# One quad of edges in four loaded from GpSimd's queue instead of SP's, in a graph layer on one core

## The chip, the core and the metric

The kernel runs on one core of a Trainium2 chip. Its time is the device time of one execution, in microseconds (us), taken as the median of several runs. Profiles come from one further execution, recorded by the hardware profiler.

## What is computed

The layer updates 12,500 nodes of 128 features. 200,000 edges of 128 features each are summed into the node that the edge points to (`dst`, sorted ascending), and a three-layer perceptron with a closing LayerNorm runs on every node:

```
agg = segment_sum(edge_attr, dst, num_segments=12500)      # 200000 x 128 -> 12500 x 128
h   = relu(layernorm(x))
h   = concat([h, agg]); h = relu(h @ W1 + b1); h = relu(h @ W2 + b2); h = h @ W3 + b3
out = x + layernorm(h) * ln_w + ln_b
```

All of it is fp32. The edges are 102.4 MB of the 116.5 MB that move.

## The kernel before

**Quads.** The edges are read once, in order, in 130 quads (`QUADS`) of 1,536 edges. A quad is 786,432 bytes and is loaded by two transfers of 384.0 KB (`load_quad`, line 344), each in rows of 1,536 bytes, into one of eight slots of `ring` (`RING = 8`). Quad q lies in slot q modulo 8. Each slot has its own semaphore, `edges_loaded[slot]`, which rises by 32 for a whole quad.

**What is done with a quad.** TensorE multiplies its rows with a one-hot matrix of VectorE (`seg`, line 497, 24 matmuls), which sums the edges of each node inside windows of 32. ScalarE copies the sums (`copy_part`). GpSimd makes a placement matrix (`placement`, line 899) that says at which rows the windows lie, TensorE applies it (`put`, line 508), and VectorE adds the result to `agg` (`add`, line 1065). `place` has two buffers, so the placement of quad q waits until the put of quad q-2 is done (`pool.wait_ge(placed, q - 1)`).

**Steps.** The nodes are worked on in groups of 384. The main loop has 31 steps (`STEPS`). Step i takes four quads, 4i+6 to 4i+9 (`AHEAD = 6`), and layers 1 to 3 of node group i between them: TensorE runs layer 1 on the sums, then seg and put of one quad, layer 2, seg and put, layer 3, seg and put, the x part of the next layer 1, seg and put, and the transposes of the group two ahead. The put that follows seg of quad q is that of quad q-1. The loop of each engine is written out by hand in that order, and the engines meet by semaphores alone.

**The queues.** SP issues every load of edges and of x and nearly all stores, in program order on one queue. In a step it issues the x rows of group i+4 (192.0 KB, line 339), then four quads, 4i+14 to 4i+17, each as `reload`: a wait until the quad that held the slot has gone through seg (`seg_done >= q - 7`), then the two transfers. From step i = 3 on it adds after each quad a store of 24.0 KB (`store_part`, line 379, 13 groups in eighths); the other groups are stored at the end, two at a time (line 384). ScalarE issues only the weights at the start and the last small pieces of the output.

**GpSimd.** It has issued no transfer so far. In a step it copies the window bases of four quads (`rows_of`, line 890), makes four placements, and adds a bias to x of group i+2 (`bias_x`, line 907). At the start it zeroes `agg` (line 884). Its step reads:

```
rows_of(4 * i + AHEAD, 4, True)
for k in range(4):
    placement(4 * i + AHEAD + k, k, k, i + 2)
if more_x:
    bias_x(i + 2)
```

Of the kernel before, what the change touches and what calls it, by code (L numbers as in the profile page):

```python
# [38 lines left out]
HALF = QC // 2  # L39
# [23 lines left out]
RING = 8  # L63
HALF_RING = RING // 2
# [14 lines left out]
AHEAD = 6  # L79
# [3 lines left out]
STEPS = GROUPS - 1  # L83
ROUNDS = (STEPS - 3) // 2
STORED_EARLY = 13
WTS = 6 * 16


def gnn_kernel(nc, x, dst, edges, w1, b1, w2, b2, w3, b3, lnw, lnb, out):
    assert CHUNKS * NODES_PER_CHUNK - SLACK >= TAIL_BASE and GROUPS == 32 and QUADS == 4 * STEPS + AHEAD and LAST_P * LAST_PER == LAST_N and LAST_P <= P and TOP_QUADS * QC == (ROWT - 1) * P and 0 < FIRST_OF_LAST <= LROW and RC * RP == REST  # L90
    with ExitStack() as ctx:
# [3 lines left out]
        def sem(name):  # L95
            return ctx.enter_context(nc.semaphore(name))
# [111 lines left out]
        edges_loaded = [sem(f"edges_loaded{k}") for k in range(RING)]  # L208
        onehot_ready = sem("onehot_ready")
        seg_done = sem("seg_done")  # L210
# [8 lines left out]
        pool_went_on = sem("pool_went_on")  # L219
# [40 lines left out]
        def half_of_edges(q, k):  # L260

            return edges[bass.ds(q * QUAD + k * (QUAD // 2), QUAD // 2), :].rearrange("(s p j) f -> p s (j f)", p=P, j=PER)

        def ring_slot(k):
            return ring[:, k, :].rearrange("p (s e) -> p s e", s=QC)
# [53 lines left out]
        with nc.Block() as block:  # L319
# [3 lines left out]
            def _(sp):  # L323
# [11 lines left out]
                def load_x(g, par, before):  # L335

                    if not (isinstance(before, int) and before == 0):
                        sp.wait_ge(x_loaded[par], 16 * before)
                    sp.dma_start(xg(g), group_rows(x, g)).then_inc(x_loaded[par], 16)  # L339

                def load_quad(q, slot):

                    for k in range(2):
                        sp.dma_start(ring_slot(slot)[:, k * HALF:(k + 1) * HALF, :], half_of_edges(q, k)).then_inc(edges_loaded[slot], 16)  # L344
# [4 lines left out]
                load_x(0, 0, 0)  # L349
                load_x(1, 1, 0)  # L350
                sp.dma_start(tail_e[:, :, :], edges[TAIL0:EDGES, :].rearrange("(p j) f -> p j f", j=PER)).then_inc(tail_loaded, 16)
                for q in range(1, HALF_RING):
                    load_quad(q, q)
                load_x(2, 0, 1)
                for q in range(HALF_RING, RING):
                    load_quad(q, q)
                load_x(3, 1, 1)

# [14 lines left out]
                def store_part(g, k):  # L373

                    p0, p1 = k * PIECE, (k + 1) * PIECE
                    if k == 0:
                        sp.wait_ge(out_ready, g + 1)
                    rows = out[bass.ds(g * CHUNK + p0 * PER, (p1 - p0) * PER), :]
                    sp.dma_start(rows.rearrange("(p j) f -> p (j f)", j=PER),  # L379
                                 xs[p0:p1, bass.ds(g * CHUNK, CHUNK)]).then_inc(stored, 16)  # L380
# [6 lines left out]
                def reload(q, slot):  # L387
                    sp.wait_ge(seg_done, q - RING + 1)  # L388
                    load_quad(q, slot)

                def fast():
                    for q in range(RING, RING + AHEAD):
                        reload(q, q % RING)

                    def step(i, par, pairs, g=None, more_x=True):

                        if more_x:
                            load_x(i + XAHEAD, (par + XAHEAD) % 2, pairs + (par + XAHEAD) // 2)
                        for k in range(4):
                            reload(4 * i + RING + AHEAD + k, (4 * par + AHEAD + k) % RING)  # L400
                            if g is not None:
                                store_part(g, 4 * (1 - par) + k)

                    step(0, 0, 0)
                    with sp.Fori(0, ROUNDS - STORED_EARLY) as t:
                        step(2 * t + 1, 1, t)
                        step(2 * t + 2, 0, t + 1)
                    with sp.Fori(ROUNDS - STORED_EARLY, ROUNDS - 1) as t:
                        g = t - (ROUNDS - STORED_EARLY)
                        step(2 * t + 1, 1, t, g)  # L410
                        step(2 * t + 2, 0, t + 1, g)
                    t, g = ROUNDS - 1, STORED_EARLY - 1
                    step(2 * t + 1, 1, t, g)
                    step(2 * t + 2, 0, t + 1, g, more_x=False)
                    pairs = (GROUPS - 2 - STORED_EARLY) // 2
                    for k in range(pairs):
                        store_two(STORED_EARLY + 2 * k)
                    for g in range(STORED_EARLY + 2 * pairs, GROUPS - 1):
                        store(g)
                    store_top(TOP_PARTS[:1])  # L420
                    store_last(GROUPS + 1, LAST_PARTS[:1])
                    singles = TOP - STORED_EARLY - 2 * pairs
                    sp.wait_ge(stored, 16 * (PIECES * STORED_EARLY + pairs + singles + len(TOP_PARTS) + len(LAST_PARTS)))
# [35 lines left out]
            def _(pe):  # L459
# [114 lines left out]
                def fast():  # L574
                    pe.wait_ge(wts_loaded, WTS)
                    pe.wait_ge(tail_loaded, 16)
# [70 lines left out]
                def general():  # L647
                    pe.wait_ge(wts_loaded, WTS)
                    pe.wait_ge(zeros_ready, 1)
# [49 lines left out]
            def _(act):  # L699
# [95 lines left out]
                def fast():  # L795
                    act.wait_ge(wts_loaded, WTS)
                    for q in range(2):
# [49 lines left out]
                def general():  # L847
                    act.wait_ge(wts_loaded, WTS)

# [26 lines left out]
            @block.gpsimd  # L876
            def _(pool):
                kw = dict(allow_small_or_imprecise_dtypes=True)
                nc.gpsimd.iota(iota[:, :], [[1, BANK]], base=0, channel_multiplier=0, **kw)
                nc.gpsimd.iota(pidx[:, :], [[0, 1]], base=0, channel_multiplier=1, **kw)  # L880
                nc.gpsimd.iota(turn[:, :], [[P * NODES_PER_CHUNK, ROWT]], base=-SLACK, channel_multiplier=NODES_PER_CHUNK,
                               **kw).then_inc(iotas_ready, 1)
                pool.wait_ge(widx_ready, 1)
                nc.gpsimd.memset(agg[:, :], 0.0).then_inc(agg_zeroed, 1)

                def rows_of(q, n, made):

                    if made:
                        pool.wait_ge(place_ready, q)
                    nc.gpsimd.tensor_copy(rows_at[:, 0:n], row_at[:, bass.ds(q, n)]).then_inc(rows_ready, 1)  # L890

                def placement(q, par_q, k, count, free=True):

                    if k == 0:
                        pool.wait_ge(rows_ready, count)
                    if free:
                        pool.wait_ge(placed, q - 1)
                        pool.sem_inc(pool_went_on, 1)
                    nc.gpsimd.tensor_scalar(place[:, par_q % 2, :], iota[:, 0:P], rows_at[:, k:k + 1], None,  # L899
                                            ALU.is_equal).then_inc(place_ready, 1)  # L900

                def bias_x(g):

                    rows, per = shape(g)
                    pool.wait_ge(h_ready, nth(g))
                    v = xg(g).rearrange("p (j f) -> p j f", j=per)
                    nc.gpsimd.tensor_tensor(v, v, lnbs[0:rows, :].unsqueeze(1).to_broadcast([rows, per, D]), ALU.add  # L907
                                            ).then_inc(x_biased, 1)

                pool.wait_ge(vecs_ready, 1)  # L910
                bias_x(LAST)

                def fast():
                    rows_of(0, AHEAD, False)
                    for q in range(2):
                        placement(q, q, q, 1, free=False)
                    bias_x(0)
                    bias_x(1)
                    for q in range(2, AHEAD):
                        placement(q, q, q, 1)  # L920

                    def step(i, more_x=True):
                        rows_of(4 * i + AHEAD, 4, True)
                        for k in range(4):
                            placement(4 * i + AHEAD + k, k, k, i + 2)
                        if more_x:
                            bias_x(i + 2)

                    with pool.Fori(0, STEPS - 1) as i:
                        step(i)  # L930
                    step(STEPS - 1, more_x=False)

                def general():
                    with pool.Fori(0, GROUPS) as g:
                        bias_x(g)

                branch(pool, fast, general)


            @block.vector  # L940
            def _(dve):
# [140 lines left out]
                def center_w3():  # L1082

                    dve.wait_ge(wts_loaded, WTS)
                    dve.wait_ge(vecs_ready, 1)
# [211 lines left out]
```

## Time and profile before

| | |
|---|---|
| median of 3 runs | 314.19 us (314.14 to 315.0) |
| the profiled execution | 314.22 us |
| its span in the trace | 312.4 us |
| TensorE busy | 280.1 us, 90% of the span |
| VectorE, ScalarE, GpSimd busy | 75%, 50%, 43% |
| moved | 116.50 MB, mean 373 GB/s |

The span is the time from the first to the last instruction in the trace; 1.8 us of the profiled execution lie outside it. TensorE's mean granted clock is 0.979 of full speed. DMA shares are of the core's 16 DMA engines; packets that overlap on one engine are counted twice, so a share can pass 100%.

### The profile page before, as it was taken

The page shows a single profiled execution, that of the slowest core. Times are in us where ns is not written, and L with a number is a line of the kernel's source. Part 1 is how long each engine was busy: PE and PEld are TensorE (multiplying, and loading weights), DVE is VectorE, ACT ScalarE, POOL GpSimd, SP SyncE. Part 2 cuts the span into 40 slices and gives each one's busy share as a digit, 9 for nine tenths or more (in the row PEclk, how much of TensorE's full clock was granted, in tenths as well). Part 3 has the DMA queues.
Part 4 walks back from the last instruction along what each step waited for, and adds up shares of the span by engine and source line. Part 5 has one row for each costly group of instructions (what it writes and reads, how often), then busy time and mean ns, then how long its engine had stood idle before and what let it go on. Part 6 is the DMA issues. An engine that isn't in the chain of part 4 may idle for free.

```text
span 312.4 us, 12913 instructions
## 1 busy us (share of the span) xinstructions
PE 280.1 (90%) x3955; PEld 182.3 (58%) x3955; DVE 233.1 (75%) x879; ACT 156.8 (50%) x413; POOL 134.0 (43%) x203
## 2 busy tenths in 40 slices
PE   2959999999999999999999999999999999999992
PEld 0746666656666666666556656565556565655671
DVE  4954777788787778777788777777787777777754
ACT  1442445555555545455555544545545545455533
POOL 7735334444444344444444443334444433444510
PEclk9976999999999999999999999999999999999998
DMA  7999999999999999999999999999999999999996
GB/s 237 342 377 373 373 373 372 372 376 383 383 383 383 383 383 384 383 383 384 383 383 383 383 383 382 384 384 383 382 383 383 383 383 383 384 382 384 384 392 217
DMA packets 83284, 116.50 MB, mean 373 GB/s; under 512 B 7116, under 2 KB 83272, under 8 KB 83272
## 3 DMA queue, kind: packets, MB, share of 16 engines
q1 hardware_dynamic: 82368, 116.06, 103.9%
q10 hardware_dynamic: 904, 0.28, 0.4%
q8 instruction: 6, 0.10, 0.1%
q14 instruction: 6, 0.05, 0.0%
HBM read 109.92 MB, written 6.40 MB: 372 GB/s over the span
## 4 chain that ended last, share of the span: by engine, by line
SPq 36%; PE 28%; issue 13%; DVE 11%; ACT 5%; DMA 4%; ACTq 1%; DVEq 1%
SPq L344 19%; SPq L379 13%; PE part_ps L497 10%; PE place_ps L508 7%; DVE onehot L973 4%; PE hid_ps L531 4%; ACT h L736 4%; PE hid_ps L541 3%; DMA ring<-in_edge_attr 3%; SPq L339 2%; DVE agg L1065 1%; DMA dst_i<-in_dst 1%; DVE x_mv L954 1%; DVE x_shift L966 1%; SPq L388 1%
## 5 line engine op out<-in xcount | busy, mean ns | idle before, releaser
L899 POOL TENSOR_SCALAR place<-iota,rows_at 128x128 f32<-128x128 f32 x130 | 84.4, 650 | 136.3 <-PE place_ps L508 127.8
L497 PE MATMUL part_ps<-ring,onehot 128*32 128x128 f32 x3120 | 113.7, 280 | 7.5 <-DMA ring<-in_edge_attr 3.2
L497 PEld LDWEIGHTS part_ps<-ring,onehot 128*32 128x32 f32 x3120 | 78.6, 110 | 66.1 <-issue 40.1
L1065 DVE TENSOR_TENSOR agg<-place_ps,agg 128x128 f32 x130 | 37.8, 291 | 58.6 <-PE place_ps L508 56.4
L508 PE MATMUL place_ps<-place,part 128*128 128x128 f32 x260 | 64.0, 329 | 2.9 <-ACT part L722 2.9
L973 DVE TENSOR_TENSOR onehot<-iota,local_t 128x768 f32<-128x768 f32 x65 | 62.4, 961 | 0.1
L736 ACT ACTIVATE h<-xs,x_shift,x_rstd 128x128 f32 (+2 forms) x98 | 41.3, 483 | 32.8 <-DVE x_shift L966 32.6
L508 PEld LDWEIGHTS place_ps<-place,part 128*128 128x128 f32 x260 | 39.5, 191 | 30.0 <-issue 21.5
L722 ACT ACTIVATE part<-part_ps 128x128 f32<-128x128 f32 x130 | 34.6, 267 | 25.3 <-PE part_ps L497 25.3
L907 POOL TENSOR_TENSOR xs<-xs,vecs 128x384 f32 (+2 forms) x33 | 33.6, 1019 | 27.0 <-ACT h L736 27.0
L531 PE MATMUL hid_ps<-agg,w1a 128*128 (+2 forms) x64 | 28.8, 532 | 7.3 <-DVE agg L1065 7.3
L1136 DVE SCALAR_TENSOR_TENSOR xs<-z,y_rstd,xs 128x128 f32 (+2 forms) x96 | 29.6, 363 | 4.6 <-DVE y_rstd L1125 0.3
L757 ACT ACTIVATE hid<-hid_ps,b2s 128x384 f32<-128x384 f32 (+2 forms) x33 | 19.0, 577 | 25.3 <-PE hid_ps L541 25.3
L549 PE MATMUL y_ps<-w3s,hid 128*128 128x128 f32 (+1 forms) x192 | 26.8, 276 | 0.0
L541 PE MATMUL hid_ps<-hid,w2s 128*128 128x384 f32 (+2 forms) x66 | 26.7, 486 | 0.0
L751 ACT ACTIVATE hid<-hid_ps,b1s 128x384 f32<-128x384 f32 (+1 forms) x32 | 18.6, 581 | 14.6 <-PE hid_ps L531 14.6
L524 PE MATMUL hid_ps<-h_t,w1x 128*128 128x384 f32 (+1 forms) x64 | 25.9, 486 | 0.0
L744 ACT ACTIVATE h_t<-ht_ps 128x384 f32<-128x384 f32 x32 | 22.4, 701 | 4.9 <-PE ht_ps L517 4.5
L549 PEld LDWEIGHTS y_ps<-w3s,hid 128*128 128x128 f32 (+1 forms) x192 | 24.0, 191 | 0.4 <-issue 0.2
L728 ACT ACTIVATE x_std<-x_mv,eps 128x3 f32<-128x3 f32 (+1 forms) x33 | 9.8, 296 | 25.7 <-DVE x_mv L954 25.7
L946 DVE BATCH_NORM_STATS2 x_stats<-xs 128x6 f32 (+2 forms) x98 | 22.1, 280 | 0.6 <-issue 0.6
L1097 DVE BATCH_NORM_STATS2 y_stats<-y 128x6 f32<-128x128 f32 x93 | 20.8, 279 | 0.0
(103 smaller groups left out, 203.9 us busy)
## 6 DMA issues: line engine op xcount, KB each, us to landing
ring<-in_edge_attr SPq DMA_DIRECT2D x260, 384.0 KB, 8.2
xs<-in_x SPq DMA_DIRECT2D x32, 192.0 KB, 7.6
out_x<-xs SPq DMA_DIRECT2D x8, 384.0 KB
out_x<-xs SPq DMA_DIRECT2D x104, 24.0 KB
dst_i<-in_dst SPq DMA_DIRECT2D x1, 768.0 KB
out_x<-xs SPq DMA_DIRECT2D x2, 192.0 KB
tail_e<-in_edge_attr SPq DMA_DIRECT2D x1, 192.0 KB, 5.1
out_x<-xs SPq DMA_DIRECT2D x1, 168.0 KB
```

What stands on the lines that cost most here:

```text
L344: sp.dma_start(ring_slot(slot)[:, k * HALF:(k + 1) * HALF, :], half_of_edges(q, k)).then_inc(edges_loaded[slot], 16)
L379: sp.dma_start(rows.rearrange("(p j) f -> p (j f)", j=PER), xs[p0:p1, bass.ds(g * CHUNK, CHUNK)]).then_inc(stored, 16)
L497: last = nc.tensor.matmul(part_ps[par_q % 2][s * WIN:(s + 1) * WIN, 0:D], onehot[:, oct_par, first + s, j, :], e[:, s, j * D:(j + 1) * D], ...
L508: nc.tensor.matmul(place_ps[par_q % 2][:, 0:P], part[0:rows, par_q % 2, :], place[0:rows, par_q % 2, :], start=True, stop=True).then_inc(p ...
L531: nc.tensor.matmul(layer1_bank(g)[:, 0:n], w1a[:, :], agg[:, bass.ds(first(g), n)], start=False, stop=True).then_inc(hid1_done, 1)
L541: nc.tensor.matmul(hid2_ps[:, 0:n], w2s[:, :], hid1[:, 0:n], start=True, stop=True).then_inc(hid2_done, 1)
L549: last = nc.tensor.matmul(y_ps[0:rows, j * D:(j + 1) * D], hid2[:, j, 0:rows], w3s[:, :], start=True, stop=True)
L722: nc.scalar.activation(part[0:rows, par_q % 2, :], part_ps[par_q % 2][0:rows, 0:D], ACT.Copy).then_inc(part_copied, 1)
L736: last = nc.scalar.activation(h[0:rows, j, :], xg(g, j), ACT.Relu, bias=x_shift[0:rows, j:j + 1], scale=x_rstd[0:rows, j:j + 1])
L899: nc.gpsimd.tensor_scalar(place[:, par_q % 2, :], iota[:, 0:P], rows_at[:, k:k + 1], None, ALU.is_equal).then_inc(place_ready, 1)
L973: nc.vector.tensor_tensor(onehot[:, par % 2, :, :, :], iota[:, 0:WIN].unsqueeze(1).unsqueeze(1).to_broadcast([P, OCT, PER, WIN]), local_t[ ...
L1065: nc.vector.tensor_tensor(v, place_ps[par_q % 2][:, 0:P], v, ALU.add).then_inc(added, 1)
```

## The change

Every fourth quad, those with q = 3 modulo 4, is issued by GpSimd on its own queue; they lie in slots 3 and 7. At the start GpSimd issues quads 3 and 7 after the zeroing of `agg`, and SP leaves them out. Quad 11 follows GpSimd's first six placements. In each step up to i = 28 GpSimd issues quad 4i+15 between the third placement and the fourth, after the same wait on `seg_done` that SP had. SP keeps the other three quads, x and the stores, in the old order. GpSimd's loop covers two steps a turn, since the slot alternates; its last three steps are written out, and the last two of them load nothing. Nothing is computed in another way.

```diff
--- before.py
+++ after.py
@@ -83,6 +83,7 @@
 STEPS = GROUPS - 1
 ROUNDS = (STEPS - 3) // 2
 STORED_EARLY = 13
+POOL_TURN = 1
 WTS = 6 * 16
 
 
@@ -349,10 +350,10 @@
                 load_x(0, 0, 0)
                 load_x(1, 1, 0)
                 sp.dma_start(tail_e[:, :, :], edges[TAIL0:EDGES, :].rearrange("(p j) f -> p j f", j=PER)).then_inc(tail_loaded, 16)
-                for q in range(1, HALF_RING):
+                for q in range(1, HALF_RING - 1):
                     load_quad(q, q)
                 load_x(2, 0, 1)
-                for q in range(HALF_RING, RING):
+                for q in range(HALF_RING, RING - 1):
                     load_quad(q, q)
                 load_x(3, 1, 1)
 
@@ -390,14 +391,16 @@
 
                 def fast():
                     for q in range(RING, RING + AHEAD):
-                        reload(q, q % RING)
+                        if q % HALF_RING != HALF_RING - 1:
+                            reload(q, q % RING)
 
                     def step(i, par, pairs, g=None, more_x=True):
 
                         if more_x:
                             load_x(i + XAHEAD, (par + XAHEAD) % 2, pairs + (par + XAHEAD) // 2)
                         for k in range(4):
-                            reload(4 * i + RING + AHEAD + k, (4 * par + AHEAD + k) % RING)
+                            if k != POOL_TURN:
+                                reload(4 * i + RING + AHEAD + k, (4 * par + AHEAD + k) % RING)
                             if g is not None:
                                 store_part(g, 4 * (1 - par) + k)
 
@@ -883,6 +886,15 @@
                 pool.wait_ge(widx_ready, 1)
                 nc.gpsimd.memset(agg[:, :], 0.0).then_inc(agg_zeroed, 1)
 
+                def load_quad(q, slot):
+
+                    for k in range(2):
+                        pool.dma_start(ring_slot(slot)[:, k * HALF:(k + 1) * HALF, :], half_of_edges(q, k)
+                                       ).then_inc(edges_loaded[slot], 16)
+
+                for q in (HALF_RING - 1, RING - 1):
+                    load_quad(q, q)
+
                 def rows_of(q, n, made):
 
                     if made:
@@ -919,16 +931,28 @@
                     for q in range(2, AHEAD):
                         placement(q, q, q, 1)
 
-                    def step(i, more_x=True):
+                    def reload(q, slot):
+
+                        pool.wait_ge(seg_done, q - RING + 1)
+                        pool.sem_inc(pool_went_on, 1)
+                        load_quad(q, slot)
+
+                    def step(i, par, load=True, more_x=True):
                         rows_of(4 * i + AHEAD, 4, True)
                         for k in range(4):
                             placement(4 * i + AHEAD + k, k, k, i + 2)
+                            if load and k == POOL_TURN + 1:
+                                reload(4 * i + RING + AHEAD + POOL_TURN, (4 * par + AHEAD + POOL_TURN) % RING)
                         if more_x:
                             bias_x(i + 2)
 
-                    with pool.Fori(0, STEPS - 1) as i:
-                        step(i)
-                    step(STEPS - 1, more_x=False)
+                    reload(RING + HALF_RING - 1, HALF_RING - 1)
+                    with pool.Fori(0, ROUNDS) as t:
+                        step(2 * t, 0)
+                        step(2 * t + 1, 1)
+                    step(STEPS - 3, 0)
+                    step(STEPS - 2, 1, load=False)
+                    step(STEPS - 1, 0, load=False, more_x=False)
 
                 def general():
                     with pool.Fori(0, GROUPS) as g:
```

## Rows read from the trace of the kernel before

**Rows 1.** The page: the DMA queues, HBM traffic, and the edge transfers' time to landing

```profile
q1 hardware_dynamic: 82368, 116.06, 103.9%
HBM read 109.92 MB, written 6.40 MB: 372 GB/s over the span
ring<-in_edge_attr SPq DMA_DIRECT2D x260, 384.0 KB, 8.2
```

**Rows 2.** Busy time by stretch; last columns are TensorE's clock, DMA share, GB/s

```profile
50.00:60.00 10.00, 9.57 (x147) 6.38 (x147) 8.00 (x28) 5.45 (x14) 4.12 (x7) 1.00 1.06 372
...
100.00:140.00 40.00, 38.01 (x565) 24.69 (x563) 31.33 (x119) 21.46 (x56) 17.50 (x29) 1.00 1.06 383
...
220.00:260.00 40.00, 36.83 (x534) 23.20 (x532) 30.82 (x118) 21.20 (x56) 17.48 (x28) 1.00 1.06 383
```

**Rows 3.** Who waited for whom, 200 to 290 us: total, times, longest

```profile
PEld part_ps L497 <- DMA ring<-in_edge_attr: 14.4, 20, 0.7
```

**Rows 4.** Timeline of GpSimd: `bias_x`, once a step (start us, duration us)

```profile
159.31 1.01 POOL L907 TENSOR_TENSOR xs<-xs,vecs 128x384 f32 x1 [0.78 <-ACT h L736]
...
176.40 1.01 POOL L907 TENSOR_TENSOR xs<-xs,vecs 128x384 f32 x1 [0.73 <-ACT h L736]
...
292.94 1.07 POOL L907 TENSOR_TENSOR xs<-xs,vecs 128x384 f32 x1 [0.46 <-ACT h L736]
```

**Rows 5.** Timeline of SP: issues of quads and stores, mid-kernel and at the end

```profile
151.69 0.97 SPq L344 DMA_DIRECT2D ring<-in_edge_attr  x2
152.88 0.36 SPq L379 DMA_DIRECT2D out_x<-xs  x1
...
282.95 0.93 SPq L344 DMA_DIRECT2D ring<-in_edge_attr  x2
...
288.11 1.12 SPq L379 DMA_DIRECT2D out_x<-xs  x1
...
291.35 0.94 SPq L344 DMA_DIRECT2D ring<-in_edge_attr  x2
```

**Rows 6.** DMA, 4 to 16 us: queues (packets, MB, share); issues (KB, us to landing)

```profile
q1 hardware_dynamic: 2898, 3.84, 95.4%
q10 hardware_dynamic: 868, 0.26, 9.4%
...
ring<-in_edge_attr SPq DMA_DIRECT2D x12, 384.0 KB, 9.6
...
w1x<-in_L_gnn_W ACTq DMA_DIRECT2D x1, 64.0 KB, 4.8
```

**Rows 7.** Timeline of TensorE near the end: seg of quads 122 and 124

```profile
286.17 0.86 PE L497 MATMUL part_ps<-ring,onehot 128*32 128x128 f32 x24
...
290.39 0.86 PE L497 MATMUL part_ps<-ring,onehot 128*32 128x128 f32 x24 [0.25 <-DMA ring<-in_edge_attr]
```

**Rows 8.** The chain that ended last, its end in order of time (quads 125, 126)

```profile
283.42 8.95 DMA ring<-in_edge_attr
...
292.42 0.86 PE part_ps L497 x24
...
295.10 0.79 PE part_ps L497 x24
```

**Rows 9.** Timelines of GpSimd and TensorE: third and fourth placement, the puts that need them

```profile
156.04 0.61 POOL L899 TENSOR_SCALAR place<-iota,rows_at 128x128 f32<-128x128 f32 x1 [1.25 <-PE place_ps L508]
157.93 0.60 POOL L899 TENSOR_SCALAR place<-iota,rows_at 128x128 f32<-128x128 f32 x1 [1.27 <-PE place_ps L508]
...
162.03 0.49 PE L508 MATMUL place_ps<-place,part 128*128 128x128 f32 x2
...
163.89 0.38 PE L508 MATMUL place_ps<-place,part 128*128 128x128 f32 x1
```

**Rows 10.** Timeline of GpSimd at the start: zeroing of `agg` and the next operation

```profile
2.56 10.77 POOL L884 MEMSET agg<- 128x12800 f32 x1 [0.99 <-DVE widx L993]
17.97 0.73 POOL L907 TENSOR_TENSOR xs<-xs,vecs 127x256 f32<-127x256 f32 x1 [4.63 <-ACT h L736]
```

## Prediction, made before the changed kernel ran

> **What bounds the kernel now.** I read the page first, then the stretches, the waits, the timelines of GpSimd and SP, and the end of the chain. The page says that SP's queue carries nearly everything and that its packets take 103.9% of the engines' span [rows 1]. By stretch the DMA share is 1.06 from 50 us on, and it never falls [rows 2]. The rate is 372 GB/s before the stores begin and 383 GB/s after, and the reader should see that these are one read rate: a step reads 8 x 393,216 + 196,608 = 3.34 MB, the stores of a step are 98,304 bytes, and 383 x 3.34 / 3.44 = 372. HBM read over the whole span gives 109.92 MB / 312.4 us = 352 GB/s, start and end included. So I take reads at 372.5 GB/s as the ceiling of these transfers: a quad takes 786,432 / 372,500 = 2.11 us, a step 8.97 us.
>
> TensorE is the other bound. GpSimd's `bias_x` marks the steps [rows 4]: 159.31 to 176.40 is two steps of 8.55 us, 176.40 to 292.94 is 13 steps of 8.96. Up to there TensorE took quads faster than they were read, so it lived on a stock of landed quads, which shrank by 0.43 us a step and was gone near 176 us. From there it waits once or twice a step for an edge transfer, 14.4 us in twenty times on the weight-load side between 200 and 290 us [rows 3]. The end of the chain agrees: a transfer of 8.95 us lands at 292.37, and from there it is TensorE's own work with quads 125 to 129 [rows 8].
>
> SP is not the bound, though it fills the chain. Mid-kernel a quad costs it 0.97 us and a store 0.36 [rows 5]. Near the end, where its code has no loop and costs less, one store takes 1.12 us, and issues 282.95 to 291.35 are four quads at 2.10 us each [rows 5], the same 2.11 as the read rate. The issue is held back until the queue has room; SP's time stretches to fill the gap.
>
> **The change, part by part.**
>
> SP's side: two edge issues less in a step, 0.97 us and some gap. Work that hides it: the wait for room in the queue, which only grows. Worth 0. If the read rate were no ceiling, SP's saved microsecond would be the gain; that is part of the faster rival.
>
> Bytes, rows and semaphores are the same. Term: 0.
>
> Rate with two queues: no row shows GpSimd's queue. The nearest is the start, where ScalarE's queue (q10) is active beside SP's [rows 6]. In 12 us they moved 3.84 and 0.26 MB, 342 GB/s together. At 372.5 the 3.84 MB alone need 10.3 us, so 0.26 MB in 868 small packets took the other 1.7 us: the second queue got its share out of the first one's, and nothing was gained by having two. That stretch also holds small packets, so it does not measure a loss. I take the rate as unchanged. Bounds: 342 GB/s in that stretch is 8% less, but if the 868 packets of 512 bytes and less explain it, the loss is 0; upward, edge packets alone at share 1.06 leave no idle engine [rows 2], but I can't exclude 2 to 3%, since the stores travelled free in the same queue, so the engines can do more than 372.
>
> By a rule, several issuers gain nothing: the Trainium skill (DMA: Bandwidth & Descriptors, section Issuing engines are not separate DMA queues) says that transfers of all issuers run on the same 16 engines and that several issuers save only sequencer time. By that rule the rate term is 0; the trace agrees as far as it goes [rows 6].
>
> GpSimd's issues. The trace has no transfer issued there. From below, SP's issue of one transfer, half of 0.97, is 0.49 us [rows 5]; as a middle, GpSimd's own pass over 128 x 384 elements takes 1.01 [rows 4]. I take about 1.1 us each, 2.2 us a step. What covers it: the third placement ends at 156.65, the fourth starts at 157.93 after the put it waits for, and is needed by the put at 162.03 [rows 9]; so two issues may take 162.03 - 0.61 - 156.65 = 4.8 us. Behind them stand the fourth placement (0.6), `bias_x` (1.0), `rows_of` and its gaps (0.7), and the first placement of the next step, 0.8, needed by the put at 163.89: 163.89 - 3.1 - 156.65 = 4.1 us. So each issue may take 2.1 us and cost nothing. `bias_x` is wanted two steps later. The wait in front of the issues (`seg_done >= 4i+8`) holds nothing up: the third placement already waited for put 4i+6, which TensorE runs after seg 4i+7. Cost 0; beyond 2.1 us per issue it is two times the excess in each of 29 steps.
>
> The start: four issues between the end of the zeroing, 13.33, and the next operation at 17.97 [rows 10], room for 1.16 us each. Quad 3 then lands by 25 us even at the 9.6 us of SP's transfers [rows 6], with quads 0 to 2 to be worked on before it. Cost 0, upper end 0.5.
>
> The order of landing. This is the term I count. Today quads land in the order in which TensorE takes them. After the change quad 4i+15 is issued about 1 + 2 x 1.1 us after seg of quad 4i+7, eight quads ahead. It need not stand behind SP's backlog: ScalarE's `w1x` landed in 4.8 us in the stretch in which SP's edge transfers took 9.6 [rows 6], against 8.2 in the median [rows 1]. So GpSimd's quad lands early and sits in the ring while the read rate it used is missing from SP's quads, which TensorE needs first. The sum of bytes at any time is the same, so the last quad, 129, lands when it does today: quad 125 at 292.37 [rows 8] plus 4 x 2.11 = 300.8. But the quads before it land later. Quad 127 is the last of GpSimd's. When 126 lands, only 128 and 129 are still missing: 300.8 - 2 x 2.11 = 296.6. Today TensorE starts seg 126 at 295.10 [rows 8]. Delay 1.5 us. When 122 lands, 123 is there and 127 is under way, so 6 down to 5 quads are missing: 288.1 to 290.3. Today seg 122 starts at 286.17 [rows 7]. Delay 2.0 to 4.1 us. TensorE can win back next to nothing from there, about 0.4 us at the one wait that is left, at quad 124 [rows 7]. At that time 127 has only begun, so I take the low end: 2.0 us. Bounds: 0, if GpSimd's packets do stand behind SP's, and 4.1.
>
> Sum against the profiled execution: 314.22 + 2.0 = 316.2 us. Its own time is the median of the runs but for 0.03 us, so the forecast for the median is 316.2. A difference below 0.3%, 0.9 us, can't be told from none here.
>
> **Rivals.**
>
> 1. No change. The early quad does not harm, since SP's quads still come in time, or GpSimd's packets queue behind SP's; or the rate rises by just under 1% and pays for it. 314.2. For it: the ring holds eight quads. Against it: TensorE has no stock left after 176 us.
>
> 2. Faster, by the read rate alone. Two queues keep more reads under way on each engine. Each per cent takes 2.9 us from the 292 us of loading, against the 2.0 of the order; it decides from a rise of 0.7% (1% to pass the measurement). At 2% it is 316.2 - 5.8 = 310.4. It ends where TensorE's own pace binds: 13 x (8.96 - 8.55) = 5.4 us, 308.8. For it: the stores ride free. Against it: rows 6.
>
> 3. Slower read rate. GpSimd's packets cost the engines more than SP's. 1% less is 316.2 + 2.9 = 319.1, 2% less 322. No row shows either.
>
> 4. GpSimd becomes the bound. At 3 us an issue the excess is 2 x 0.9 = 1.8 us a step, 29 steps, minus the 0.4 a step that TensorE waits anyway from 176 us on: some 45 us, 360 us. It decides from 2.1 us. The other way in is a port that VectorE holds while GpSimd writes its descriptors.
>
> The Trainium skill (SBUF — State Buffer, section SBUF: two separate sides) warns of just that for transfers issued on GpSimd when VectorE runs copies or scalar operations in its two-port modes. In this kernel's loop VectorE runs two-tensor adds, statistics and multiply-adds, no plain copy or one-tensor scalar operation, so by that page rival 4 gets nothing from it; no run here shows it.
>
> **How the numbers follow.** Order of landing, 315.3 to 318.3: 0.40. No change: 0.16. Faster read rate: 0.26. Slower read rate: 0.13. GpSimd bound: 0.05. Slower is 0.40 + 0.13 + 0.05 = 0.58, within 0.3% 0.16, faster 0.26. Predicted 316.2. The range takes the slower rate to 2%, 322, and the faster to just short of its floor, 309.3; 0.05 for GpSimd and some 0.1 at the ends stay out. The likeliest case alone has 315.3 to 318.3.
>
> **What the profile after should show.** GpSimd's issues near 1.1 us each and its placements as long before their puts as the sum says. SP's stores longer than today. DMA share 1.06 and 383 GB/s as before; any other value decides between rivals 2 and 3. GpSimd's transfers land in 4 to 6 us, SP's in more than 8.2. The first waits of TensorE for the ring come earlier than 176 us, and are longer, in front of quads 4i+2 or so; quad 122 starts about 2 us later. I am wrong if the rate moves by a per cent, if GpSimd's issues pass 2.1 us, or if its transfers wait like SP's.

## Result and the profile after

The changed kernel takes 317.55 us in the median of 4 runs (317.17 to 318.16) against 314.18 before: a ratio of 1.0103, 95% interval 1.0079 to 1.0127. That is 3.4 us more by the medians, 3.2 by the ratio; 316.2 was forecast. The differences below are ratios times 314.2. Its profiled execution took 317.29 us with a span of 315.5, against 314.22 and 312.4.

The page first: queues (packets, MB, share), HBM traffic, and the edge transfers of the two issuers (KB, us to landing).

```profile
q1 hardware_dynamic: 64960, 90.89, 81.0%
q0 software_dynamic: 7168, 25.17, 21.5%
...
HBM read 109.92 MB, written 6.40 MB: 369 GB/s over the span
...
ring<-in_edge_attr SPq DMA_DIRECT2D x196, 384.0 KB, 9.4
ring<-in_edge_attr POOLq DMA_DIRECT2D x64, 384.0 KB, 7.1
```

The bytes are those of [rows 1]. A quarter of the edges lands in 7.1 us, the rest now needs 9.4 instead of 8.2: GpSimd's transfers overtake SP's, and SP's pay. By stretch (last columns clock, DMA share, GB/s):

```profile
0.00:10.00 10.00, 3.35 (x11) 1.54 (x12) 5.51 (x15) 1.98 (x3) 8.24 (x8) 1.00 0.82 256
10.00:20.00 10.00, 8.16 (x116) 6.25 (x114) 9.02 (x36) 5.18 (x13) 7.25 (x6) 1.00 1.04 355
...
100.00:140.00 40.00, 37.75 (x543) 24.30 (x541) 30.87 (x120) 21.28 (x55) 23.72 (x37) 1.00 1.06 382
...
220.00:260.00 40.00, 36.22 (x532) 23.54 (x536) 30.73 (x117) 20.37 (x54) 24.62 (x37) 1.00 1.06 382
```

The DMA engines are as full as in [rows 2], at 382 instead of 383 GB/s. TensorE is already less busy at 100 to 140 us (37.75 against 38.01 us), where it was not yet short of quads before. Its timeline shows since when. In front of one quad in four TensorE now waits for the ring; these are the first and the fifteenth of these waits, one a step, and they go on to 275.45:

```profile
131.40 0.86 PE L500 MATMUL part_ps<-ring,onehot 128*32 128x128 f32 x24 [0.36 <-DMA ring<-in_edge_attr]
...
257.45 0.86 PE L500 MATMUL part_ps<-ring,onehot 128*32 128x128 f32 x24 [0.46 <-DMA ring<-in_edge_attr]
```

The steps are 126.05 / 14 = 9.00 us long here. In the kernel before, the same view has its first such wait at 182.57 us, and steps of 8.98. The end of the chain, in order of time:

```profile
283.73 0.45 SPq L345
284.23 11.20 DMA ring<-in_edge_attr
...
295.47 0.86 PE part_ps L500 x24
...
298.22 0.79 PE part_ps L500 x24
...
304.99 0.88 PE place_ps L511 x4
```

It is the chain of [rows 8] with one landing changed: the transfer that lets seg of quad 125 start lands at 295.43 instead of 292.37. It was issued 0.8 us later (284.23 instead of 283.42) and was 11.20 us under way instead of 8.95. All behind it takes as long as before.

GpSimd, in one step and at the start:

```profile
157.50 0.60 POOL L911 TENSOR_SCALAR place<-iota,rows_at 128x128 f32<-128x128 f32 x1 [1.26 <-PE place_ps L511]
158.27 1.50 POOL L892 DMA_DIRECT2D ring<-in_edge_attr  x2 [0.17 <-issue]
159.95 0.61 POOL L911 TENSOR_SCALAR place<-iota,rows_at 128x128 f32<-128x128 f32 x1 [0.17 <-PE place_ps L511]
160.77 1.31 POOL L919 TENSOR_TENSOR xs<-xs,vecs 128x384 f32 x1 [0.21 <-ACT h L739]
```

```profile
13.40 3.12 POOL L892 DMA_DIRECT2D ring<-in_edge_attr  x4
18.22 0.72 POOL L919 TENSOR_TENSOR xs<-xs,vecs 127x256 f32<-127x256 f32 x1 [1.69 <-ACT h L739]
```

An issue costs GpSimd 0.75 us. The fourth placement starts 0.18 us behind the issues, where GpSimd sat idle for 1.27 us in [rows 9]; the view names TensorE's put as what it waited for, but between 62 and 133 us the same placement starts within 0.06 us of the issues with no wait named, so there it is the issues that it follows. It is in time all the same: the list of TensorE's waits has none for a placement. At the start the four issues end 1.69 us before the next operation.

### The profile page after: what moved, and what is told of

Same layout as the page of the kernel before. It is cut to its first block, busy times and chain, and to the rows that moved or that the text cites. A ratio compares the mean times of both kernels' runs of the same rounds, so it can differ in the third digit from the quotient of the medians.

```text
span 315.5 us, 12889 instructions
## 1 busy us (share of the span) xinstructions
PE 279.5 (89%) x3955; PEld 181.8 (58%) x3955; DVE 234.2 (74%) x879; ACT 157.0 (50%) x413; POOL 186.0 (59%) x267
## 3 DMA queue, kind: packets, MB, share of 16 engines
q0 software_dynamic: 7168, 25.17, 21.5%
## 4 chain that ended last, share of the span: by engine, by line
SPq 44%; PE 16%; DMA 15%; issue 12%; DVE 8%; ACT 2%; POOL 1%; DVEq 0%; ACTq 0%; POOLq 0%
SPq L345 21%; SPq L380 18%; DMA ring<-in_edge_attr 14%; PE part_ps L500 7%; PE place_ps L511 4%; SPq L340 3%; PE hid_ps L534 2%; DVE onehot L997 2%; PE hid_ps L544 2%; ACT h L739 2%; DMA dst_i<-in_dst 1%; DVE xs L1160 1%; POOL xs L919 1%; PE y_ps L552 1%; SPq L389 1%
## 5 line engine op out<-in xcount | busy, mean ns | idle before, releaser
L892 POOL DMA_DIRECT2D ring<-in_edge_attr x64 | 48.1, 752 | 6.2 <-issue 4.6
L919 POOL TENSOR_TENSOR xs<-xs,vecs 128x384 f32 (+2 forms) x33 | 37.2, 1127 | 12.4 <-ACT h L739 12.4
```

The source lines that it names most:

```text
L892: pool.dma_start(ring_slot(slot)[:, k * HALF:(k + 1) * HALF, :], half_of_edges(q, k)).then_inc(edges_loaded[slot], 16)
```

## Experiments

Each was timed against the kernel before on the same chip, in five rounds. All compute the full result. Two theories were to be told apart. **A, order of landing:** a quad that lies in the ring ahead of its turn delays the quads before it by the time its bytes took, and this costs where TensorE has no stock, above all in the last quads. **B, the queue:** the second queue itself costs, by its rate or its descriptors, quad by quad.

**Where in the kernel: GpSimd only early, or only late.** Slots 3 and 7 have a second pair of semaphores for the late half, and TensorE waits for these there. GpSimd's side of the edit (SP's takes or leaves the same quads):

```diff
# e1_first_half (e2_second_half with True and False exchanged)
-    with pool.Fori(0, ROUNDS) as t:
-        step(2 * t, 0)
-        step(2 * t + 1, 1)
+    with pool.Fori(0, HALF_WAY) as t:                  # HALF_WAY = 6
+        step(2 * t, 0, load=True)
+        step(2 * t + 1, 1, load=True)
+    step(2 * HALF_WAY, 0, load=True)                   # quad 63, the last
+    step(2 * HALF_WAY + 1, 1, load=False)
+    with pool.Fori(HALF_WAY + 1, ROUNDS) as t:
+        step(2 * t, 0, load=False)
+        step(2 * t + 1, 1, load=False)
```

> GpSimd issues its quads only up to quad 63, SP issues all four from quad 67 on. Theory A, order of landing: a quad that lies in the ring early delays the quads before it by about one quad, and that costs only where TensorE has no stock of landed quads, after about 131 us, and above all at the end. Here the order is restored before that counts, so the loss of 3.4 us is nearly gone: 314.3 to 314.9 us, the rest being half of a read rate that is 0.24% lower. Theory B, the second queue itself costs (read rate, descriptor writing): the loss goes with the number of quads on it, 14 of 32 are left, so 315.7 us.

> The complement: SP issues all quads up to 66, GpSimd one in four from quad 67 on. Theory A: nearly the whole loss stays, 316.8 to 317.4 us. Theory B: half of the loss, 315.9 us.

The first half alone: ratio 1.0015 (1.0000 to 1.0031), 0.5 us. The second half alone: 1.0088 (1.0065 to 1.0111), 2.8 us. Each half has 16 of GpSimd's 32 quads (3 to 63 are 16, not the 14 of the expectation), so the loss does not go by their number; A foretold both, B neither. The end of the chain of the first-half kernel is that of the kernel before, 0.4 us later:

```profile
283.77 8.97 DMA ring<-in_edge_attr
292.78 0.86 PE part_ps L508 x24
```

**The order without a second queue.** The kernel before, SP alone, one quad in four two places early:

```diff
+    reload(RING + HALF_RING + 3, (RING + HALF_RING + 3) % RING)      # quad 15
-    for k in range(4):
-        reload(4 * i + RING + AHEAD + k, (4 * par + AHEAD + k) % RING)
+    for k, n in enumerate((0, 2, 5, 3)):
+        if n != 5 or early:                                          # not in the last step
+            reload(4 * i + RING + AHEAD + n, (4 * par + AHEAD + n) % RING)
```

> The kernel before with all loads on SP's queue, but quad 4i+19 issued before 4i+17 and 4i+18, two places early. No second queue at all. Theory A: quad 4i+18 lands one quad later than in order, which is the same delay as with GpSimd's queue, without the loss of rate: 315.7 to 316.4 us. Theory B: 314.2 us.

1.0079 (1.0057 to 1.0101): 2.5 us without any transfer from GpSimd. B falls with this. It is 0.3 to 1 us more than A said; the page of this run has two slices of 362 and 353 GB/s near 39 to 55 us where the kernel before has 373 and 372, about 0.6 us of reading lost. SP waited there for the slot of a quad that it wanted early. Chain end:

```profile
286.74 9.10 DMA ring<-in_edge_attr
295.89 0.86 PE part_ps L500 x24
```

**One quad alone.** All in order but quad 127, which SP issues before 125 and 126 (e9), or before 126 only (e10):

```diff
-    step(2 * t + 1, 1, t, g)
-    step(2 * t + 2, 0, t + 1, g, more_x=False)
+    step(2 * t + 1, 1, t, g, order=(0, 1, 2, 5, 3))                   # e10: (0, 1, 2, 3)
+    step(2 * t + 2, 0, t + 1, g, more_x=False, order=(0, 2, 3))       # e10: (1, 0, 2, 3)
```

> The kernel before, all loads on SP's queue in order, but for one quad: 127 is issued before 125 and 126. Everything up to quad 124 is untouched. Theory A: quad 125 lands when only 126, 128 and 129 are missing, 2.1 us later than in order, and TensorE has no stock there, so moving this one quad costs as much as the whole reordering: 316.0 to 316.5 us. Theory B (the cost is paid quad by quad over the kernel, or by the second queue): 314.2 to 314.3 us.

> Likewise, but 127 is issued before 126 only. Theory A: 125 lands as before, 126 lands at 296.6 us, 1.5 us after TensorE starts it today: 315.5 to 315.9 us. Theory B: 314.2 us.

e9: 1.0108 (1.0091 to 1.0126), 3.4 us; e10: 1.0047 (1.0031 to 1.0064), 1.5 us. One misplaced quad of 130, at the end, costs as much as all 32 of the change. The chains show the two landings:

```profile
285.76 9.24 DMA ring<-in_edge_attr
295.05 0.86 PE part_ps L499 x24
```

```profile
287.36 9.18 DMA ring<-in_edge_attr
...
296.59 0.86 PE part_ps L499 x24
```

In e10 the transfer lands at 296.54; the prediction's sum for quad 126 had 296.6, and 1.5 us of delay. In e9 quad 125 starts 2.6 us later than in [rows 8], not 2.1. The 0.5 us of difference has nothing to do with the misplaced quad: in that execution quad 52 already landed 0.5 us later than in the kernel before, and so did every quad up to 124. The timed runs add 0.8 us more, and for these the cause was not found out, so e9 shows that one quad costs at least its 2.1 us, and not why the timed loss is 3.4.

**How late it can be restored.** As e1, with the change of hands at quad 115 (`HALF_WAY = 12`):

> GpSimd issues its quads up to 111, SP all from 115 on: only the last four of the 32 quads go back. Theory A: quads land in order again from 115, but TensorE is 2.1 us late there and wins back 0.43 us a step over 3.7 steps, so 0.5 us of delay is left, plus 0.6 for the rate: 315.2 us, 2.3 us less than the changed kernel for four quads. Theory B: 28 of 32 of the loss is left, 317.1 us.

1.0024 (1.0009 to 1.0038), 0.8 us. Giving back the last four of GpSimd's quads removes 2.5 of the 3.2 us. TensorE catches up as it is faster than the reads, by some 0.5 us a step here: the trace has it 2.1 us late at quad 112 (265.50 against 263.44) and 1.0 us late at quad 120 (282.42 against 281.40). That 1.0 stays to the end, as the last quad lands 1.0 us late too.

**How early.** GpSimd issues quad 4i+11 in step i, behind the first placement (five ahead of use) or the third (three ahead):

```diff
-    if load and k == POOL_TURN + 1:
-        reload(4 * i + RING + AHEAD + POOL_TURN, (4 * par + AHEAD + POOL_TURN) % RING)
+    if load and k == 0:                                               # e3_latest: k == 2
+        reload(4 * i + RING + HALF_RING - 1, (4 * par + HALF_RING - 1) % RING)
```

> Quad 4i+11 behind the first placement of step i, five quads ahead of use; one quad in four on GpSimd's queue as before. With 7.1 us to landing it still lands before quads 4i+9 and 4i+10. Theory A (order of landing): what counts is only whether it lands before its neighbours, not by how much, so the loss stays, 316.8 to 317.8 us. Rival: the loss grows with the time the quad lies in the ring, and then this is halfway, 315.8 us.

> Same queue, same place in GpSimd's step (behind the third placement), but the quad issued there is 4i+11 instead of 4i+15: three quads ahead of use instead of seven. Same number of issues and bytes on GpSimd's queue. At 7.1 us to landing it lands about when its turn comes. Theory A: the order is nearly kept, the delay of some 2.2 us falls to 0 to 0.7, 314.9 to 315.6 us; if it lands after its turn, TensorE waits for it in every step and the time passes 318. Theory B: as the changed kernel, 317.5 us.

Five ahead: 1.0079 (1.0063 to 1.0096), 2.5 us. Two quads less of lead change the loss little, if at all. The expectation was off in one point: in this trace GpSimd's quad passes one of SP's quads, 4i+10, and not two (119 lands at 278.61, 117 at 275.06, 118 at 279.81). Quad 122 lands 3.0 us late, quad 125 only 0.7, but TensorE, held up at 122, still starts quad 129 2.7 us late. One quad passed costs nearly what the three of the changed kernel do. Three ahead was my miss: 1.0518 (1.0482 to 1.0553), 16 us. The branch that I had written for a quad that comes after its turn is what happened, and worse than 318. Who waited for whom, the transfers, a stretch (last number GB/s), and one quad from its issue to TensorE:

```profile
PEld part_ps L500 <- DMA ring<-in_edge_attr: 36.6, 30, 3.0
```

```profile
ring<-in_edge_attr SPq DMA_DIRECT2D x196, 384.0 KB, 6.1
ring<-in_edge_attr POOLq DMA_DIRECT2D x64, 384.0 KB, 5.9
```

```profile
100.00:140.00 40.00, 36.13 (x536) 23.72 (x536) 29.28 (x114) 19.53 (x52) 22.73 (x35) 1.00 1.05 381
```

```profile
111.64 1.50 POOL L892 DMA_DIRECT2D ring<-in_edge_attr  x2 [0.17 <-issue]
```

```profile
118.36 0.86 PE L500 MATMUL part_ps<-ring,onehot 128*32 128x128 f32 x24 [0.37 <-DMA ring<-in_edge_attr]
```

Both are quad 43, which lands at 118.31, 6.67 us after GpSimd began to issue it. TensorE works on quads 40 to 42 in that time and is done a little sooner, so it waits for this quad, and does so in nearly every step. SP's quad 44, behind it, has been in the ring since 110.03. TensorE waits for the ring from 45 us on, up to 3.0 us at a time. So its steps take 9.1 us from 45 us on, where the kernel before had 8.55 up to 176 us. SP's transfers land in 6.1 us; most likely less is under way, since GpSimd's slot stands empty for longer, SP has filled its six and must wait for TensorE. The page has 350 to 372 GB/s in its slices from 33 to 90 us and only 333 in one near the end.

**Is it GpSimd's queue?** The same quads from 15 on, at the same place of the order, from ScalarE's hardware queue (3, 7 and 11 stay with SP), and two quads in four from GpSimd:

```diff
# e6_scalar_queue
     copy_part(q + 2, AHEAD + 2)
+    if load:
+        reload(4 * i + RING + AHEAD + TURN, (4 * par + AHEAD + TURN) % RING)    # act.dma_start x2
# e8_two_in_four
-    if load and k == POOL_TURN + 1:
-        reload(4 * i + RING + AHEAD + POOL_TURN, (4 * par + AHEAD + POOL_TURN) % RING)
+    if load and k in (POOL_TURN, POOL_TURN + 1):
+        reload(4 * i + RING + AHEAD + k - 1, (4 * par + AHEAD + k - 1) % RING)
```

> The same quads at the same place of the order, issued by ScalarE on its hardware queue behind its copy of the sums of quad 4i+8; SP issues the first round and quad 11. Theory A: the same early landing and so the same delay of 2.1 us, 316.3 us if the lower read rate belongs to GpSimd's queue (383 GB/s here instead of 382), 317.3 if it comes with any second queue; up to 1 us more if two issues of 0.4 us hold up ScalarE's next copy. Theory B (GpSimd's software queue and its descriptors cost): 314.2 us.

> GpSimd issues two quads in four, 4i+14 and 4i+15, behind the second and third placement of a step. Theory A: when quad 125 lands, 126 and 127 are there and only 128 and 129 are missing, so it lands 4.2 us late instead of 2.1, and the rate is 0.5% lower, 1.4 us: 319.8 us (319 to 321). Theory B: twice the loss, 320.9 us. The stretch rate tells the price of the queue: 381 GB/s if it is GpSimd's packets, 382 if it is the second queue as such.

ScalarE: 1.0092 (1.0067 to 1.0116), 2.9 us, the changed kernel's loss without GpSimd. Two in four: 1.0190 (1.0161 to 1.0218), 6.0 us, of which A foretold 5.6 and B 6.7, so this one does not tell them apart. Its chain shows quad 125 starting at 299.60, 7.2 us late where 4.2 + 1.4 were summed. The 4.2 holds; it is the last quad that lands 3.0 us late instead of 1.4. The page of this run has two slices of 353 and 346 GB/s near 24 to 40 us, and TensorE waits for quad 17 already, at 56 us:

```profile
286.28 13.28 DMA ring<-in_edge_attr
299.60 0.86 PE part_ps L500 x24
```

For the rate, one stretch of each, 60 to 280 us: before, changed, SP alone in the other order, ScalarE, two in four.

```profile
60.00:280.00 220.00, 206.16 (x3002) 132.28 (x3000) 170.78 (x654) 115.64 (x301) 93.83 (x151) 1.00 1.06 383
```

```profile
60.00:280.00 220.00, 202.88 (x2951) 130.76 (x2949) 169.54 (x648) 114.24 (x299) 133.35 (x199) 1.00 1.06 381
```

```profile
60.00:280.00 220.00, 201.35 (x2948) 130.49 (x2947) 166.83 (x647) 114.06 (x298) 89.14 (x150) 1.00 1.06 383
```

```profile
60.00:280.00 220.00, 200.39 (x2927) 129.89 (x2931) 166.65 (x645) 114.22 (x298) 88.89 (x149) 1.00 1.06 382
```

```profile
60.00:280.00 220.00, 199.28 (x2908) 128.61 (x2910) 168.44 (x634) 111.75 (x292) 199.18 (x244) 1.00 1.05 381
```

One queue keeps 383 whatever its order; with two it is 381 or 382. The price is there with ScalarE's queue too, so it is not GpSimd's queue alone. The expectation for two in four wanted to tell the queues apart by 381 or 382; whole GB/s are too coarse for that. The bytes of the packets in the same traces give, in the same order, 382.7, 381.5, 382.5, 381.8 and 380.7 GB/s: 0.2 to 0.3% for one quad in four, about the same from either queue, and 0.5% for two.

## Why the prediction held, step by step

**The bound.** Reads at one rate, and TensorE short of quads after 176 us: right. In the kernel before, the first wait that the timeline names is at 182.57, and by the landing times TensorE starts quad 73 at 175.60, 0.04 us after it landed, and those behind it likewise.

**Order of landing, forecast 2.0 us.** The mechanism is shown: by e1 and e2 for the place, by e4 for the absence of the queue, by e10 for the size of one quad's step. The size came out near by luck. I summed for quads 126 and 122 and passed over 125, which is what the end hung on, and took 2.0 from quad 122. When 125 lands, 127 is there and only 126, 128 and 129 are missing: 300.8 - 3 x 2.11 = 294.5, 2.1 us after 292.37. Measured was 295.43, 3.06 us late. The remaining 1.0 us is in the other number of the sum: I had the last quad, 129, land when it does today, and it lands at 301.67 instead of 300.69. Quads 122 and 124 in the timeline of the changed kernel:

```profile
289.57 0.86 PE L500 MATMUL part_ps<-ring,onehot 128*32 128x128 f32 x24 [0.32 <-DMA ring<-in_edge_attr]
...
293.44 0.86 PE L500 MATMUL part_ps<-ring,onehot 128*32 128x128 f32 x24
```

They start 3.4 and 3.05 us later than in [rows 7]; 2.0 to 4.1 was the bound for 122. With the 1.0 us that all reads are late taken off, 2.4 us of order are left at quad 122, near the low end.

The same sum can be tried on every run but e3, where TensorE waits for one late quad and not for the reads as a whole. It is the quads that have landed ahead of their turn when quad 125 lands, at 2.11 us each, plus what the last quad, 129, is late (us against the kernel before, by the landing times of the profiled executions):

| run | ahead of 125 | x 2.11 | 129 late | sum | 125 late |
|---|---|---|---|---|---|
| changed kernel | 1 | 2.1 | 1.0 | 3.1 | 3.1 |
| e1, early half alone | 0 | 0 | 0.4 | 0.4 | 0.4 |
| e2, late half alone | 1 | 2.1 | 1.0 | 3.1 | 3.1 |
| e4, SP's order | 1 | 2.1 | 1.4 | 3.5 | 3.5 |
| e5, five ahead | 0 | 0 | 0.7 | 0.7 | 0.7 |
| e6, ScalarE's queue | 1 | 2.1 | 0.7 | 2.8 | 2.8 |
| e7, restored at 115 | 0 | 0 | 1.0 | 1.0 | 1.0 |
| e8, two in four | 2 | 4.2 | 3.0 | 7.2 | 7.2 |
| e9, 127 before 125 | 1 | 2.1 | 0.5 | 2.6 | 2.6 |
| e10, 127 before 126 | 0 | 0 | -0.1 | -0.1 | -0.1 |

In e5 the end does not hang on 125 but on 122, as said above.

Nor is it quads 4i+2 alone that suffer, as the prediction had it. In the changed kernel all of SP's quads from mid-kernel on are late alike (100, 101 and 102 by 2.9 to 3.0 us), since one quad of GpSimd's is always ahead of them; the named wait stands in front of quads 4i.

**Rate, forecast 0.** This is the term that was set too low. Steps of 9.00 instead of 8.98 are 0.2%, 0.6 us of the 292. The bound toward a loss held, and the sign was that of [rows 6], which I had seen and set to 0.

**Start, forecast 0 to 0.5.** 256 and 355 GB/s in the first two stretches, 258 and 360 in the same view before: 70 KB less in 20 us, 0.2 us. The sum of the three is 2.1 + 0.6 + 0.2 = 2.9 of 3.06 us in the traces. The two small terms are near what one execution differs from the next: the last quad of e9 lands 0.5 us later, that of e10 0.1 us earlier than in the kernel before, all three with one queue.

**GpSimd's issues, forecast 1.1 us each at no cost.** 0.75 us, no cost. `bias_x` takes 1.13 instead of 1.02 in the mean, 1.31 at most, and nobody waits for it. Rival 4 never came near. The prediction's list of VectorE's work leaves out two reciprocals on 128 x 3 elements a step; beside all of it the 64 issues took 0.72 to 0.95 us.

**SP's freed time, forecast worth nothing.** It is. While GpSimd's last quad is on its way, one store of SP's takes 2.92 us, by SP's timeline:

```profile
283.73 1.09 SPq L345 DMA_DIRECT2D ring<-in_edge_attr  x2
284.87 2.92 SPq L380 DMA_DIRECT2D out_x<-xs  x1
```

**Time to landing.** I gave GpSimd's transfers 4 to 6 us; they take 7.1. It changed nothing, since seven quads of lead are some 15 us. For three quads of lead it decides: there a transfer lands in 5.9 us, but a quad, two transfers issued one behind the other, needed 6.67 us, and TensorE's own pace with a stock is 3 x 8.55 / 4 = 6.4 us for three quads.

**The rivals.** No change and a faster rate are out by the measured interval. A slower rate is the smaller part of the loss: 0.2 to 0.3%, and not the per cent or two of rival 3.

## What to carry to other kernels

When a kernel is bound by its reads and takes them in order, the issue order is the landing order it needs; a second queue that overtook the first added no bandwidth here but spent it on the wrong transfer. The delay is the early bytes over the read rate, it is hidden as long as the consumer has a stock, and at the end a single misplaced quad costs all of it. Before giving a share of the loads to another engine, ask whether the first issuer's time stretches to fill the gap: if it does, it had none to save.

## What the runs showed that I had not expected

GpSimd's queue moves 25.17 MB in 7,168 packets, 3.5 KB each, where SP's packets carry 1.4 KB on average; its share per MB is 0.85% against 0.89%. Yet the rate did not rise.

The stores add 3% to the bytes and next to nothing to the time: 372 GB/s of reads alone, 383 with stores. In the kernel before, a step's reads land in 8.96 us from quad 16 to 20, before the first store, and in 8.99 from quad 60 to 124.

Issued three quads ahead of use, one quad in four costs 16 us, and five ahead 2.5: too late is dearer than too early, as TensorE then waits for that quad in nearly every step, with SP's quads behind it landed long before.
